# Preparing the experts' weights inside the attention steps of a two-layer transformer kernel on one core

## The chip, the core and the metric

One core of a Trainium2 chip runs the whole program in one launch. The metric is device time in microseconds (us). TensorE is written PE (its weight loads PEld), VectorE DVE, ScalarE ACT, GpSimd POOL; SyncE (SP) issues most DMAs.

## The reference

Input x is 4 x 1024 x 256 (4096 tokens). Each of two layers does a modulated layer norm, attention with 16 heads of 16, a gated residual, a second modulated norm, eight experts of which each token takes two, and a gated residual.

```
h = layernorm(x) * (1 + ca) + sa
x = x + ga * attention(h)        # layer 0: window of 64, q and k rms-normed; layer 1: causal, rope
h = layernorm(x) * (1 + cb) + sb
x = x + gb * experts(h)
# layer 0, for each expert i (H = 1024), tokens with i in their top 2:
W1 = w1_v[i] / max(|row|, 1e-12) * w1_g[i] ;  W2 likewise
out += silu(xm @ W1.T + b1[i]) @ W2.T + b2[i]
# layer 1 (H = 512): gelu(z @ W1 + b1) @ W2 + b2, weighted by the top-2 probabilities
```

The weights are multiplied in two f16 parts: `hi = f16(w)` and `lo = f16(w - hi)`. Layer 0's row norms are not put into the weights but into scales `s1` (on the hidden units) and `s2` (on the outputs).

## The kernel before

`build` runs, for each layer, `project` (norm, q, k, v to DRAM), `attend`, `out_project` and `moe`. Each stage is one block: its engines' programs start together and the next block begins when all have ended. Inside a block each engine follows its own written order and waits on semaphores.

`attend` does 16 steps (4 batches x 4 groups of heads). A list `plan`, made from the sizes, fixes the order inside a step: score matmuls ("st"), maxima of the next step's scores ("max"), the transposes "nmT" (the maxima) and "oT" (the output), and the products with V ("pv"). PE writes "max", "nmT" and "oT" into a ring of two PSUM slots, `pmx`, that DVE empties (`dve_max` L832, `dve_nm`, `dve_norm`); PE may fill a slot only when DVE has read what was in it two entries before. ACT takes the exponentials (L880). SP issues, per step, 13 loads of Q, K and V (L687, L689), after the last "pv" of the step before, and then three small DMAs (L695) that carry the maxima of the next step; that step's scores wait for these. POOL does nothing in the steps.

`moe` runs `moe_input` (norm, router logits, the input z to DRAM in two f16 parts, L1419; ACT writes the first part at L1459 into two buffers, each free again when its store has landed), `moe_route` (who goes where, in chunks of a one-hot product), `moe_weights`, `moe_tiles` (39 tiles of 256 rows) and `moe_combine`.

`moe_weights` is a stage of its own. SP loads an expert's W1 and W2 in f32, ACT copies them to f16 (`hi`) and, in layer 0, squares them (L1238, L1243); PE sums the squares over partitions with a matrix of ones (L1269, L1277); DVE forms `lo` (L1292, L1294) and the scales. Everything stays in `self.w1`, `self.w2`, `self.s1`, `self.s2` in SBUF. Then `moe_tiles` gathers its first rows (L1797), transposes them (L1827), and DVE's copy of them (L1920) lets the first product (L1841) begin.

## Time and profile before

| | |
|---|---|
| three runs | 2458.42, 2462.68, 2467.8 us; median 2462.68 |
| the profiled execution | 2462.16 us, span 2460.3 us |
| busy over the span | PE 74%, DVE 64%, ACT 46%, POOL 25% |
| granted TensorE clock, mean | 0.845 of full speed |

The span is the time from the first to the last instruction of that one execution. The busy shares are means over stages that are bound by different things, so they don't say what a change in one stage is worth; the timeline of that stage does.

### The profile page before, as it was taken

To read this page: it belongs to the slowest core of one execution; us is meant where nothing else is said; L and a number is where in the kernel's file an instruction comes from. 1 tells how busy PE (TensorE), PEld (TensorE's weight loads), DVE (VectorE), ACT (ScalarE), POOL (GpSimd) and SP (SyncE) were. 2 spreads that over 40 slices of the span, in tenths; PEclk is the share of its full clock that TensorE was granted. 3 is DMA by queue.
4 is the path that set the end of the run, shared out by engine and by line. 5 is a ranking of instruction groups with operands and counts; after the bars stand their busy time and mean duration, and the time that the engine had idled before them with its cause. 6 is when DMAs were issued, how large, how long until landed. Compare 5 with 4: busy or idle time off the path is not lost. (4 is left out here: it accounts for less than half of the span.)

```text
span 2460.3 us, 53785 instructions
## 1 busy us (share of the span) xinstructions
PE 1823.6 (74%) x17980; PEld 1306.3 (53%) x17981; DVE 1570.8 (64%) x2726; ACT 1123.6 (46%) x2192; POOL 608.6 (25%) x518
## 2 busy tenths in 40 slices
PE   4994989843688999999159689989887142199990
PEld 2773555643577999899135234433335132177770
DVE  3653777577355566566359589989865797355554
ACT  2662555442553434444035267767784441233332
POOL 0442000023003333333326500000000233155654
PEclk8996999955668999999579789999999555599995
DMA  4324332010531111111423421211100111422226
GB/s 138 115 108 137 100 100 78 16 61 29 203 105 61 50 46 49 47 47 43 154 81 147 154 58 46 65 48 46 46 3 16 48 42 38 146 75 80 80 75 219
DMA packets 160130, 196.79 MB, mean 80 GB/s; under 512 B 23188, under 2 KB 122676, under 8 KB 159460
## 3 DMA queue, kind: packets, MB, share of 16 engines
q1 hardware_dynamic: 144792, 153.72, 19.6%
q0 software_dynamic: 14976, 40.91, 5.5%
q8 instruction: 100, 1.64, 0.3%
q14 instruction: 58, 0.48, 0.1%
q10 hardware_dynamic: 204, 0.05, 0.0%
HBM read 125.97 MB, written 67.67 MB: 79 GB/s over the span
## 5 line engine op out<-in xcount | busy, mean ns | idle before, releaser
L832 DVE TENSOR_REDUCE a_mx<-a_pmx 128x4 f32<-128x512 f32 (+1 forms) x448 | 457.6, 1057 | 88.8 <-PE a_pmx L783 65.5
L880 ACT ACTIVATE a_probs<-a_pst 128x512 f32<-128x512 f32 (+2 forms) x832 | 421.9, 562 | 202.1 <-PE a_pst L799 165.4
L1841 PE MATMUL m_ph<-m_xT,m_w 128*128 128x256 f16 x2808 | 323.2, 275 | 20.8 <-DVE m_xT L1920 20.8
L1855 PE MATMUL m_py<-m_w,m_hh 128*128 x2808 | 319.3, 273 | 0.2 <-issue 0.2
L1841 PEld LDWEIGHTS m_ph<-m_xT,m_w 128*128 x2808 | 273.1, 99 | 63.7 <-issue 30.5
L1855 PEld LDWEIGHTS m_py<-m_w,m_hh 128*128 128x128 f16 x2808 | 268.3, 98 | 35.3 <-issue 2.4
L812 PE MATMUL a_pacc<-a_probs,a_V 128*32 128x256 f32 (+4 forms) x3456 | 247.2, 368 | 0.7 <-ACT a_probs L880 0.3
L1803 POOL DMA_INDIRECT m_y_d<-m_y,m_give x156 | 154.3, 989 | 345.4 <-DVE m_y L1916 329.7
L1926 DVE CAST m_hh<-m_hf 128x512 f16<-128x512 f32 x234 | 101.9, 436 | 210.0 <-ACT m_hf L1891 108.9
L1889 ACT ACTIVATE m_hf<-m_ph,m_b,m_s 128x256 f32<-128x256 f32 x312 | 157.2, 561 | 126.6 <-PE m_ph L1841 117.2
L1797 POOL DMA_INDIRECT m_xr<-z_d,m_take x156 | 152.1, 975 | 224.2 <-issue 221.9
L771 PE MATMUL a_pmx<-a_Ks,a_Qs 48*128 48x192 f16 (+4 forms) x1280 | 167.2, 309 | 52.0 <-DMA a_V<-v_d 36.3
L1380 POOL MEMSET m_eps<- 128x1 f32 x2 | 0.2, 103 | 792.4 <-POOLq L1057 792.4
L793 PE MATMUL a_pst<-a_Qs,a_Ks 51*128 51x192 f16 (+4 forms) x1280 | 157.8, 301 | 32.2 <-ACT a_probs L880 13.7
L1928 DVE TENSOR_TENSOR m_hh<-m_hf,m_hh 128x512 f16<-128x512 f32 x234 | 162.1, 693 | 8.0
L793 PEld LDWEIGHTS a_pst<-a_Qs,a_Ks 51*128 51x128 f16 x1280 | 44.2, 94 | 181.7 <-ACT a_probs L880 139.0
L555 PE MATMUL p_pqk<-p_hT,p_w 128*128 128x512 f32 x256 | 125.9, 615 | 0.0
L812 PEld LDWEIGHTS a_pacc<-a_probs,a_V 128*32 128x32 f32 x3456 | 71.0, 109 | 69.3 <-issue 33.8
L1827 PE MATMUL m_pt<-ident_h,m_xr 128*128 128x128 f16 x624 | 49.3, 224 | 75.3 <-DMA m_xr<-z_d,m_take 75.3
L1891 ACT ACTIVATE m_hf<-m_ph,m_b 128x256 f32<-128x256 f32 x156 | 63.4, 473 | 90.2 <-PE m_ph L1841 88.9
L524 PE MATMUL p_ptr<-ident,p_xn 128*128 128x128 f32 x128 | 27.5, 299 | 97.1 <-DVE p_xn L448 97.1
L771 PEld LDWEIGHTS a_pmx<-a_Ks,a_Qs 48*128 48x128 f16 x1280 | 52.7, 96 | 84.9 <-issue 45.5
(227 smaller groups left out, 3097.4 us busy)
## 6 DMA issues: line engine op xcount, KB each, us to landing
v_d<-p_vt SPq DMA_DIRECT2D x16, 1024.0 KB, 4.6
parts_d<-p_part SPq DMA_DIRECT2D x64, 256.0 KB, 2.6
a_V<-v_d SPq DMA_DIRECT2D x32, 512.0 KB, 3.9
m_got<-m_y_d SPq DMA_DIRECT2D x32, 512.0 KB, 5.8
a_Qs<-parts_d SPq DMA_DIRECT2D x192, 64.0 KB, 2.2
a_Ks<-parts_d SPq DMA_DIRECT2D x192, 64.0 KB, 2.2
z_d<-m_zh SPq DMA_DIRECT2D x16, 512.0 KB, 2.9
m_st<-L_w1T SPq DMA_DIRECT2D x8, 1024.0 KB, 4.8
```

What stands on the lines that cost most here:

```text
L555: mm = nc.tensor.matmul(pqk[:, q % 2, :], w[:, c, ch * P:(ch + 1) * P], hT[:, half, c, :], start=(c == 0), stop=(c == DC - 1))
L771: mm = nc.tensor.matmul(pmx[:, slot, r, n * cols:(n + 1) * cols], Qs[par][ROW2 * r:ROW2 * r + KROWS, p, i * P:(i + 1) * P], Ks[par][ROW2 * ...
L793: mm = nc.tensor.matmul(pst[:, bank(hg, 2 * n + r), off:off + q1 - q0], Ks[par][ROW2 * r:ROW2 * r + KAUG, p, j * P:(j + 1) * P], Qs[par][R ...
L812: mm = nc.tensor.matmul(pacc[32 * h:32 * h + 32, q0 - c * HALF:q1 - c * HALF], V4[par][:, j, h, :], src, start=(v, k) == half_start[c], st ...
L832: nc.vector.tensor_reduce(mx[:, part, :, ps[0]:ps[0] + len(ps), i], src, AX.X, ALU.max).then_inc(m_done, 1)
L880: nc.scalar.activation(probs[:, (hg * NV + g) % NGB, 2 * a + u % 2, 0:w], pst[:, bank(hg, u), 0:w], ACT.Exp, scale=HD ** -0.5).then_inc(ex ...
L1797: pool.indirect_dma_start(xr[:, j % 2, a, :], None, self.z_d[layer][:, :], bass.IndirectOffsetOnAxis(ap=self.take[:, 2 * j + a:2 * j + a + ...
L1803: pool.indirect_dma_start(self.y_d[:, :], bass.IndirectOffsetOnAxis(ap=self.give[:, 2 * j + a:2 * j + a + 1], axis=0), y[:, j % 2, a, :], ...
L1841: mm = nc.tensor.matmul(ph[:, (G * par + g) % 4, q * ROWS:(q + 1) * ROWS], self.w1[:, bass.ds(e, 1), c, wp, m * P:(m + 1) * P].rearrange(" ...
L1855: mm = nc.tensor.matmul(py[:, a, 0:D], hh[:, par, m, hp, a * P:(a + 1) * P], self.w2[:, bass.ds(e, 1), m, wp, :].rearrange("p a n -> p (a ...
L1889: nc.scalar.activation(hf[:, g % 2, q, :], ph[:, (G * par + g) % 4, q * ROWS:(q + 1) * ROWS], func, bias=col(self.b1), scale=col(self.s1)) ...
L1928: nc.vector.tensor_tensor(lo, hf[:, g % 2, :, :], hi, ALU.subtract).then_inc(lo_done, 1)
```

## The change

`moe_weights` is gone. The preparation is spread over the 16 steps of each layer's attention, one of an expert's two matrices per step (even steps W1, odd steps W2): SP loads it in f32 (`load_w`) into `wst`, POOL casts it to `hi`, and `lo` is formed by POOL in layer 1 and by DVE in layer 0, in two halves at items ("lo", 0) and ("lo", 1) of the plan. Both parts are stored to a new DRAM tensor `w_d` (`store_w`). In layer 0, ACT squares the matrix in four pieces after exponentials 3, 5, 7 and 9 of the step, POOL adds the pieces up (one addition of 1024 elements for W1; 1024, 512 and 256 for W2), PE sums over partitions in a new ring item ("sum") of the next step (8 products for W1, one for W2), and DVE copies the sums to `s1` or `s2`.

`moe_input` loads the prepared parts, 16 DMAs, ahead of its own stores of z; `x_d` is stored there too. `moe_route` works in 8 chunks with two buffers each, instead of 4 chunks with one each, to make room. `moe_tiles` turns the sums into scales at its start (root, maximum, reciprocal, product). The weights are 16.8 MB in layer 0 and 8.4 MB in layer 1.

```diff
@@ attend: the plan and the new helpers
+            sum_at = (3, 0) if layer == 0 else None
...
+                if (g, a) == sum_at:
+                    plan.append(("sum",))
+                if layer == 0 and g in (4, 6):
+                    plan.append(("lo", g // 2 - 2))
...
+            def pe_sum(pe, slot, s, hg):
+                par = hg % 2
+                pe.wait_ge(w_acc, s + 1)
+                if par == 0:
+                    for m in range(self.NH):
+                        mm = nc.tensor.matmul(pmx[:, slot, 0, m:m + 1], wsq[:, par, m * P:(m + 1) * P], w_ones[:, 0:1], ...)
+                else:
+                    mm = nc.tensor.matmul(pmx[:, slot, 0, 0:D], w_ones[:, :], wsq[:, par, 0:D], start=True, stop=True)
+                mm.then_inc(w_sum, 1)
...
+            def dve_lo(dve, hg, s, i):
...
+                dve.wait_ge(w_hi, s + 1)
+                nc.vector.tensor_tensor(lo, src, hi, ALU.subtract).then_inc(w_lo, 1)
@@ attend: ACT, in act_step after the exponential u
+                    if layer == 0 and u in (3, 5, 7, 9):
...
+                        nc.scalar.activation(wsq[:, hg % 2, piece], wst[:, hg % 2, piece], ACT.Square).then_inc(w_sq, 1)
@@ attend: POOL, one step
+                        pool.wait_ge(w_in[par], 32 * b + 16 * (hg // 2) + 16)
...
+                        nc.gpsimd.tensor_copy(hi, src).then_inc(w_hi, 1)
+                        pool.wait_ge(w_hi, s + 1)
+                        if layer == 1:
+                            nc.gpsimd.tensor_tensor(lo, src, hi, ALU.subtract).then_inc(w_lo, 1)
+                        if layer == 0:
+                            pool.wait_ge(w_sq, 4 * s + 4)
...
+                                nc.gpsimd.tensor_tensor(wsq[:, par, 0:n], wsq[:, par, 0:n], wsq[:, par, n:2 * n], ALU.add)...
@@ attend: SP, one step (store_w waits for w_lo of the step before)
                     def step(b, hg, last):
                         s = SETS * b + hg
+                        if used(s):
+                            store_w(*((b, hg - 1) if hg else (b - 1, SETS - 1)))
+                        if not last or hg < SETS - 1:
+                            if layer == 0 and used(s):
+                                sp.wait_ge(w_sq, 4 * s)
+                            load_w(*((b, hg + 1) if hg < SETS - 1 else (b + 1, 0)))
                         if not last or hg == 0:
                             if used(s):
                                 sp.wait_ge(pv_done, NX * s)
...
+                    store_w(B - 1, SETS - 1)
+                    for par in range(2):
+                        sp.wait_ge(w_out[par], 16 * STEPS // 2)
@@ moe
-                self.moe_weights(layer)
@@ moe_input: SP, ahead of run(sp, slot)
+                    for e in range(EXPERTS):
+                        for w, dst in enumerate((self.w1, self.w2)):
+                            sp.dma_start(dst[:, e, :, :, :]..., self.w_d[layer][e, w, :, :]).then_inc(self.w_in, 16)
+                    if not twice:
+                        sp.dma_start(self.x_d..., self.x[:, 0:EXPERTS, :]).then_inc(x_out, 16)
@@ moe_route
-            N2, CH = 2 * TILES, 4
+            N2, CH = 2 * TILES, 8
@@ moe_tiles: DVE, ahead of turned(0, 0); before it ACT takes the roots of s1 and s2
+                        for i, (sc, g) in enumerate(((self.s1, g1), (self.s2, b2))):
+                            dve.wait_ge(root, i + 1)
+                            nc.vector.tensor_scalar(sc[:, :, :], sc[:, :, :], 1e-12, None, ALU.max)...
+                            nc.vector.reciprocal(sc[:, :, :], sc[:, :, :])...
+                            nc.vector.tensor_tensor(sc[:, :, :], sc[:, :, :], g[:, :, :], ALU.mult).then_inc(scaled, 1)
```

On DVE, in the second attention step of layer 0 (`a_mx<-a_pmx` is a maximum, `a_nmp` the transposed maxima, `attn` the output), the order before:

```order
L850 TENSOR_TENSOR a_nmp<-a_nmr,a_nmp 32x128
L832 TENSOR_REDUCE a_mx<-a_pmx 128x4 x2
L858 RECIPROCAL a_rden<-a_pmx 128x16
L861 TENSOR_TENSOR attn<-a_pmx,a_rden 128x4x64
L832 TENSOR_REDUCE a_mx<-a_pmx 128x4 x4
```

and now:

```order
L900 TENSOR_TENSOR a_nmp<-a_nmr,a_nmp 32x128
L882 TENSOR_REDUCE a_mx<-a_pmx 128x4
L876 TENSOR_TENSOR a_wpt<-a_wst,a_wpt 128x4x256
L882 TENSOR_REDUCE a_mx<-a_pmx 128x4
L908 RECIPROCAL a_rden<-a_pmx 128x16
L911 TENSOR_TENSOR attn<-a_pmx,a_rden 128x4x64
L882 TENSOR_REDUCE a_mx<-a_pmx 128x4
L876 TENSOR_TENSOR a_wpt<-a_wst,a_wpt 128x4x256
L882 TENSOR_REDUCE a_mx<-a_pmx 128x4 x3
```

The two halves of `lo` (L876) stand between maxima that read different PSUM slots.

On SP, at the start of layer 0's `moe_input`, before:

```order
L1408 DMA m_gg<-L_ffn_gate_g 128x8
L1410 DMA m_rows<-mod_d 128x1024 x2
L1419 DMA z_d<-m_zh 128x4x512 x3
```

and now:

```order
L1372 DMA m_gg<-L_ffn_gate_g 128x8
L1374 DMA m_rows<-mod_d 128x1024 x2
L1389 DMA m_w<-w_d 128x4096 x16
L1391 DMA x_d<-x_res 128x8x256
L1383 DMA z_d<-m_zh 128x4x512 x3
```

Seventeen transfers of 1 MB each stand ahead of the stores of z in the same queue.

On DVE, the first instructions of layer 0's `moe_tiles` (`s` is s1, then s2; `m_xT` the first tiles' rows) are now these, where before the copies of `m_xT` came first:

```order
L1928 TENSOR_SCALAR s<-s 128x64
L1930 RECIPROCAL s<-s 128x64
L1932 TENSOR_TENSOR s<-s,m_g 128x64
L1928 TENSOR_SCALAR s<-s 128x2048
L1930 RECIPROCAL s<-s 128x2048
L1932 TENSOR_TENSOR s<-s,x_res 128x2048
L1914 COPY m_xT<-m_pt 128x1024 x2
```

Six instructions, three of them over 2048 elements, moved ahead of the copies.

## Rows read from the trace of the kernel before

**Rows 1.** Windows: busy us (instructions) of PE, PEld, DVE, ACT, POOL; PEclk, DMA share, GB/s.

```profile
205.00:450.00 245.00, 195.61 (x3792) 125.17 (x3792) 154.29 (x272) 122.22 (x289) 4.40 (x3) 0.90 0.34 92
300.00:352.00 52.00, 45.12 (x881) 29.12 (x881) 35.14 (x61) 27.77 (x67) 0.00 (x0) 0.93 0.36 99
496.00:575.00 79.00, 42.58 (x196) 39.21 (x196) 55.48 (x122) 38.22 (x83) 20.48 (x13) 0.51 0.20 70
617.00:740.00 123.00, 91.76 (x384) 80.05 (x384) 57.68 (x45) 64.24 (x57) 0.20 (x1) 0.65 0.45 154
```

**Rows 2.** Timeline, ends of layer 0's weights stage: start, us, engine, line, op.

```profile
616.56 0.38 SPq L1210 DMA_DIRECT2D x_d<-x_res  x1
...
738.70 0.55 DVE L1313 RECIPROCAL m_s<-m_s 128x64 f32<-128x64 f32 x1
...
739.77 0.35 SPq L1791 DMA_DIRECT2D x_res<-L_ffn_b  x1
...
749.77 12.68 PE L1841 MATMUL m_ph<-m_xT,m_w 128*128 128x256 f16 x96
```

**Rows 3.** Timeline, ends of layer 1's weights stage.

```profile
2085.28 0.38 SPq L1204 DMA_DIRECT2D m_st<-L_ffn_W  x1
...
2136.56 0.35 SPq L1791 DMA_DIRECT2D m_b<-L_ffn_b  x1
```

**Rows 4.** Timeline of SP in a steady attention step of layer 0.

```profile
305.80 2.76 SPq L687 DMA_DIRECT2D a_Qs<-parts_d  x6
...
313.40 1.66 SPq L695 DMA_DIRECT2D a_Qs<-a_nmp  x3
318.48 2.75 SPq L687 DMA_DIRECT2D a_Qs<-parts_d  x6
```

**Rows 5.** Tile m_sq, the squares of the weights: ns min/median/max.

```profile
L1269 PE MATMUL m_pss<-m_ones,m_sq x256: 250/352/367, 627.3 to 728.0; 128*128 128x1 f32 x128
...
L1277 PE MATMUL m_pbc<-m_sq,m_ones x128: 379/634/774, 634.1 to 734.1; 128*128 128x256 f32 x128
L1238 ACT ACTIVATE m_sq<-m_st x16: 1039/1047/1057, 626.1 to 722.0; 128x1024 f32<-128x1024 f32 x16
```

**Rows 6.** Groups by line and shape: busy us, mean ns, idle before.

```profile
L1997 POOL TENSOR_TENSOR m_got<-m_got 128x1024 f32<-128x1024 f32 x8 | 20.1, 2515 | 39.9 <-DMA m_got<-m_y_d 39.9
...
L1294 DVE TENSOR_TENSOR m_w<-m_st,m_w 128x2048 f32 x8 | 18.3, 2292 | 25.5 <-ACT m_w L1244 25.5
...
L1299 DVE RECIPROCAL m_rt<-m_rt 128x256 f32<-128x256 f32 x8 | 14.0, 1753 | 0.3
...
L1294 DVE TENSOR_TENSOR m_w<-m_st,m_w 128x1024 f32 x8 | 9.8, 1225 | 26.5 <-ACT m_w L1244 26.4
...
L1297 DVE TENSOR_SCALAR m_rt<-m_rt 128x256 f32<-128x256 f32 x8 | 2.3, 294 | 9.7 <-ACT m_rt L1250 9.7
```

**Rows 7.** Timeline of the experts' input stage, layer 0.

```profile
498.30 0.91 SPq L1410 DMA_DIRECT2D m_rows<-mod_d  x2
...
514.99 2.12 POOL L1398 TENSOR_TENSOR m_zh<-m_zs,m_zh 128x1024 f16<-128x1024 f32 x1 [17.68 <-ACT m_zh L1459]
...
515.16 3.04 DVE L1541 TENSOR_TENSOR m_zs<-m_zs,m_rows 128x1024 f32<-128x1024 f32 x1
...
517.14 49.18 SPq L1419 DMA_DIRECT2D z_d<-m_zh  x8
...
528.13 1.04 ACT L1459 ACTIVATE m_zh<-m_zs 128x1024 f16<-128x1024 f32 x1
```

**Rows 8.** DMA issues: KB each, median us from issue to landing.

```profile
m_s<-L_ffn_w_g SPq DMA_DIRECT2D x1, 1024.0 KB, 12.1
x_res<-L_ffn_b SPq DMA_DIRECT2D x1, 1024.0 KB, 4.5
```

**Rows 9.** Timeline of SP in the experts' input stage, layer 1.

```profile
1909.02 0.69 SPq L1413 DMA_DIRECT2D m_lnr<-L_ffn_ln_b  x1
1943.38 88.89 SPq L1419 DMA_DIRECT2D z_d<-m_zh  x8
```

More of the change, by code:

```diff
@@ L641, in attend @@
             nm_mid = sem("nm_mid")
+            W = 2 * self.H
+            wst = sb("wst", [P, 2, W])
+            wpt = sb("wpt", [P, 2, 2 * W], F16)
+            wsq = sb("wsq", [P, 2, W]) if layer == 0 else None
+            w_ones = sb("w_ones", [P, P]) if layer == 0 else None
+            w_in, w_out = [sem("w_in0"), sem("w_in1")], [sem("w_out0"), sem("w_out1")]
+            w_set, w_hi, w_lo, w_sq, w_ch, w_acc, w_sum, w_kept = (sem(n) for n in ("w_set", "w_hi", "w_lo", "w_sq", "w_ch", "w_acc", "w_sum", "w_kept"))
             maxu = self.max_units(layer)
@@ L726, in attend @@
             assert not rest
-            ring = [n for n, item in enumerate(plan) if item[0] in ("max", "nmT", "oT")]
+            ring = [n for n, item in enumerate(plan) if item[0] in ("max", "nmT", "oT", "sum")]
             CNT = len(ring)
@@ L732, in runs @@
             def runs(item, hg, first, last):
-                if first and hg == 0 and (item == ("oT", 1) or item[0] == "pv" and item[3]):
+                if first and hg == 0 and (item in (("oT", 1), ("sum",)) or item[0] == "pv" and item[3]):
                     return False
@@ L745, in slot_free @@
                     pe.wait_ge(nmT_read, s + 2)
+                elif item[0] == "sum":
+                    pe.wait_ge(w_kept, s)
                 else:
@@ L944, in _ @@
                     pe.wait_ge(ones_in, 16 * 2 * SETS)
+                    if layer == 0:
+                        pe.wait_ge(w_set, 1)
                     def turn(b, first, last):
@@ L950, in turn @@
                             for n, item in enumerate(plan):
-                                if not runs(item, hg, first, last):
+                                if not runs(item, hg, first, last) or item[0] == "lo":
                                     continue
@@ L976, in _ @@
                     pe_oT(pe, 0, STEPS - 1, 1)
+                    if layer == 0:
+                        pe_sum(pe, 1, STEPS - 1, SETS - 1)
                 @block.vector
@@ L989, in turn @@
                             s = SETS * b + hg
-                            for n in ring:
-                                item = plan[n]
+                            for n, item in enumerate(plan):
+                                if item[0] == "lo":
+                                    dve_lo(dve, hg, s, item[1])
+                                if n not in ring:
+                                    continue
                                 if not runs(item, hg, first, last):
@@ L1008, in _ @@
                     dve_norm(dve, 0, STEPS - 1, 1, TPB * (B - 1) + 4, (SETS - 1) * HG * HD)
+                    if layer == 0:
+                        dve_sum(dve, 1, B - 1, SETS - 1)
                 @block.scalar
@@ L1424, in _ @@
                         sp.wait_ge(zh_out[h], 16 * B)
+                    if not twice:
+                        sp.wait_ge(x_out, 16)
                 @block.scalar
@@ L1645, in _ @@
                         act.wait_ge(col_set, c + 1)
-                        nc.scalar.activation(colv[:, span(c), 0, :], colh[:, span(c), :], ACT.Copy, scale=places[:, 0:1]).then_inc(val1, 1)
+                        if c >= 2:
+                            act.wait_ge(inv_ch, c - 1)
+                        nc.scalar.activation(colv[:, c % 2, :, 0, :], colh[:, c % 2, :, :], ACT.Copy, scale=places[:, 0:1]).then_inc(val1, 1)
                 @block.tensor
@@ L1778, in moe_tiles @@
             ys_ready = sem("ys_ready")
+            g1 = sb("g1", [P, EXPERTS, NH]) if layer == 0 else None
+            g_in, root, scale_ch, scaled = (sem(n) for n in ("g_in", "root", "scale_ch", "scaled"))
             pt = self.ps(ctx, T + "pt", [P, 2, 1024], F16)
@@ L1877, in _ @@
                     act.sem_inc(act_done, 8)
+                    if layer == 0:
+                        nc.scalar.activation(self.s1[:, :, :], self.s1[:, :, :], ACT.Sqrt).then_inc(root, 1)
+                        nc.scalar.activation(self.s2[:, :, :], self.s2[:, :, :], ACT.Sqrt).then_inc(root, 1)
+                        act.wait_ge(scaled, 1)
                     def hidden(j, par):
```

261 lines of the change are left out of this document (100 added, 161 removed).

## The prediction

> **What bounds the kernel now.** The busy shares of the page are read first, and set aside: they mix stages. The windows by stage say more. In layer 0's weights stage (617 to 740 us) PE is busy for 92 of 123 us, but at a granted clock of 0.65 and on nothing but the sums of squares; the DMA share is 0.45 [rows 1]. No tile's product can begin in it. Its bounds are read from the timeline: SP's first issue at 616.56, the next stage's first issue at 739.77, so 123.2 us [rows 2]. Layer 1's stage lasts from 2085.28 to 2136.56, 51.3 us [rows 3]. These 174.5 us stand in series with everything and go; the question is what comes back elsewhere.
>
> Layer 0's attention is where the work goes. A step lasts 12.7 us (SP's first load at 305.80 and again at 318.48 [rows 4]). In 52 us of it PE is busy for 45.1 (87%), DVE for 35.1 (68%, 8.6 us a step), ACT for 27.8 (53%), POOL for nothing [rows 1]. PE has the least room, and it already shares two PSUM slots with DVE. Layer 1's steps only get work on POOL.
>
> **The change part by part.** All times are against the profiled execution, 2462.16 us with a span of 2460.3; the median of the three runs, 2462.68, is the same for this purpose.
>
> *Attention, layer 0, per step.* PE's sums: for W1 eight products with one column, for W2 one of 256 columns. The least durations of their kinds, 250 and 379 ns, are those at the higher clock [rows 5], which this stage has (0.93 [rows 1]). Eight of the first are at most 2.0 us; they overlap, so I take 1.6, and 0.5 us for the second with its weight load, a mean of 1.05, all of it on PE's path.
>
> DVE's halves: two subtractions of 1024 elements at 1.22 us [rows 6]. DVE has 4.1 us idle a step, but not where these stand. The first delays one maximum by 1.2 us and PE's maximum two ring entries later; PE is occupied with the transposes for about half of that, so I charge 0.6. ACT's last square (half of 1.05 us for 1024 elements [rows 5]) delays the same transposes by 0.5 and is in that 0.6. The second half meets POOL's additions, which can start only when the fourth square is done. What then happens is in the input stage: POOL's subtraction ran from 514.99 to 517.11, DVE's product of two SBUF tensors began at 515.16 and took 3.04 us instead of 1.2; it ended 1.1 us after POOL did [rows 7]. So the half waits for the rest of an addition of 2.5 us [rows 6], between 0 and 2.5; I take the middle, 1.2 us, and with the half itself, less the slack of the ring, 1.1 us on PE's next maximum. The Trainium skill ("SBUF — State Buffer", "SBUF: two separate sides") says that DVE with two SBUF inputs and POOL exclude each other for a whole instruction. By that rule the price is the remainder, as above; by a sharing of bandwidth, at the row's ratio of 2.5, it would be 1.8 us each time and the stage 10 us longer.
>
> Sum: 1.05 + 0.6 + 1.1 = 2.75 us a step, 44 us for 16. The stage's end waits for the last half's store, 1 MB behind DVE's last work, 4.5 us [rows 8] less the last products: 2 us. Together 46. Bounds: from below 17 us (only PE's sums are felt; less is excluded, since PE is at 87% and has more to do), from above 8 us a step (1.05, two halves of 1.22 and each a whole addition of 2.5 waited for), 128 us.
>
> What SP gets beside this is two issues a step of 0.4 us and 2.1 MB in its queue. Its chain is nearly closed already: loads from 305.80, the maxima's DMAs from 313.40 to 315.06, and in the 3.4 us until the next step's loads those DMAs land and the scores and products that wait for them run [rows 4]. The store waits for the second half, so it comes at the step's end, where SP waits for the last products anyway. I cost it at nothing as long as the step grows by 2.7 us; it is a rival below.
>
> *Attention, layer 1.* POOL casts and subtracts 1024 elements in a step; DVE's maxima read PSUM, and no row shows such an operation slowed by POOL. 0 us, up to 0.5 a step (8) for the extra issues.
>
> *Input stage, layer 0.* Sixteen loads of 1.05 MB and x_d, 17.8 MB, are issued behind the rows of 498.30, in about 8 us. Before, the first store of z was issued at 517.14, and ACT's third first-part ran at 528.13 [rows 7]; it has to wait for that store's landing, since there are two buffers. In the present trace a transfer of 1 MB issued behind three others landed after 12.1 us instead of 4.5 [rows 8]: one queue is worked off in order. The rate: the weights stage moved 154 GB/s at a share of 0.45 [rows 1], so about 340 GB/s when full. 17.8 MB then take 52 us, from 500 to 552, and the store lands at 554. With rows of 8 KB it could be somewhat faster; 400 GB/s would give 547. I take 551, 23 us behind 528, less 1 us caught up: 22. Bounds: 0 (the store passes the loads) and 30. The Trainium skill ("SBUF — State Buffer", "A bandwidth-pool intuition that's wrong (but worth ruling out)") gives about 358 GB/s for HBM; by that the loads would take 50 us and this term would be 22 to 24, an estimate that this trace neither shows nor excludes.
>
> *Input stage, layer 1.* 8.4 MB from 1909.7 take 25 us, to 1937; the first store of z was issued at 1943.38 [rows 9]. Hidden: 0 us. If that cover were gone (a rate below 250 GB/s), it would cost the difference.
>
> *Routing.* Eight chunks of half the size instead of four: the same elements, eight more instructions on each engine, a shorter tail. 0 us, -2 to +3 in each layer.
>
> *Tiles, layer 0.* The first product began 10.0 us after the stage's first issue (749.77 - 739.77 [rows 2]). Now DVE first waits for 1 MB of w2_g, issued second, landing 4.5 us later [rows 8]: 5.3 us. The scale s1 takes a reciprocal of 0.55 us [rows 2] and two small operations, 1.0. For s2, 2048 elements, the operations were seen on 256: the maximum 0.29 us, the reciprocal 1.75 [rows 6], so at most 2.4 and 14.0; the product as the subtraction over 2048, 2.29 [rows 6]. That is 18.7; with the fixed part of each counted once about 17.5. First product at 5.3 + 1.0 + 17.5 + 0.7 = 24.5 us: 14.5 later than before, at most 16. Layer 1 has no such chain. b2 now comes after the scales and lands 5 us later, under the first tile's 12.7 us of products [rows 2].
>
> The sum: 2462.2 - 174.5 + 46 + 22 + 14.5 = **2370 us**.
>
> **The rivals.** *A: the halves are absorbed.* DVE's 4.1 us of idle time take both halves and only PE's sums count: 17 + 2 us. For it: DVE waits for PE, not the other way round, in most of its gaps, and every delay of PE lets DVE catch up. Against: the idle time lies at the transposes, the halves elsewhere. 2370 - 27 = 2343.
>
> *B: the stores of z don't wait.* If what SP issued later can pass the loads, the input stage costs nothing: 2348. Against it is the landing after 12.1 us.
>
> *C: SP's queue sets the step.* The store waits for a delayed second half; store and load add 0.9 us ahead of the 13 loads, and the maxima's DMAs land behind 2.1 MB more, 6.2 us at 340 GB/s, two thirds of it not under SP's issues: 4.1. The step becomes 12.7 + 5.0: +80, not +44, and the time 2406. For it: SP's issues and the landing after them fill the step already. Against: 9.3 us of issues are room for most of the 6.2.
>
> *D: slower than before.* One chain: second half, store, load, the 13 loads, the maxima's DMAs, the scores, with nothing overlapped. Then the 6.2 us of transfers come in full on top of 12.7, and each half waits for a whole addition (5.0), 11.2 us a step, 179 for 16: 2370 - 44 + 179 = 2505. It decides from 8.5 us a step on, since 174.5 - 22 - 14.5 - 2 = 136 us are left for 16 steps. Against: as for C, and an addition is met at its start in half of the cases at most.
>
> *E: the change doesn't do what it says*, that is, the weights aren't there when the tiles begin. The loads end some 60 us before that. Nothing speaks for it.
>
> **How the numbers follow.** The forecast 0.50; A 0.23; B 0.08; C 0.14; D 0.03; E and what I don't see 0.02. A with B gives 2321, so low is 2336, which leaves out about one in ten; C sets the upper end, 2410. The forecast's own range is 2355 to 2388. About 0.5% (12 us) is what a measurement of this kernel tells from no change. All cases but D and part of the last are far beyond it: faster 0.95, within 0.5% 0.02, slower 0.03.
>
> **What would show it.** The two weights stages are gone and nothing of their length stands between routing and tiles. Layer 0's steps last 15 to 15.5 us; L876 has two kinds of durations, 1.2 us at its first place and up to 3.7 at its second. PE's idle time before the maxima's products names DVE. ACT's third first-part of z stands some 22 us later in its stage than 528.13 did, in layer 0 alone. The copies of m_xT in layer 0's tiles begin 24 us after the stage, behind a reciprocal of about 13 us. I am wrong if the step stays under 14 us (A) or passes 17 with SP late (C), if the input stage is as long as before (B), or if layer 1's steps grew.

## The result, and the profile after

The changed kernel takes 2379.04 us (median of 4 runs, 2373.74 to 2381.89) against 2463.01 us of the kernel before on the same chip: ratio 0.9656, 95% interval 0.9631 to 0.9682, so 84 us less. 2370 us were forecast, 92 us less. The profiled execution took 2377.91 us with a span of 2375.9.

Where it went, stage by stage, from SP's first issue in one stage to its first issue in the next (us; "weights" has no stage after the change):

| stage | before | after | difference | forecast |
|---|---|---|---|---|
| attention, layer 0 | 244.9 | 306.3 | +61.3 | +46 |
| experts' input, layer 0 | 73.4 | 93.7 | +20.3 | +22 |
| routing, layer 0 | 46.9 | 46.7 | -0.2 | 0 |
| weights, layer 0 | 123.2 | - | -123.2 | -123.2 |
| tiles, layer 0 | 445.7 | 459.0 | +13.3 | +14.5 |
| attention, layer 1 | 469.7 | 467.4 | -2.3 | 0 |
| input and routing, layer 1 | 179.6 | 178.6 | -0.9 | 0 |
| weights, layer 1 | 51.3 | - | -51.3 | -51.3 |
| tiles, layer 1 | 270.0 | 268.4 | -1.6 | 0 |

All terms but one came out within 3 us. Layer 0's attention grew by 15 us more than forecast; the small terms together came out 8 us lower, so that the whole is 8 to 9 us off. The windows of the kernel after (busy us and instructions of PE, PEld, DVE, ACT, POOL; PEclk, DMA share, GB/s) answer to [rows 1]:

```profile
205.00:511.00 306.00, 239.62 (x3936) 155.12 (x3936) 204.97 (x320) 155.58 (x353) 95.52 (x52) 0.83 0.63 183
300.00:352.00 52.00, 44.41 (x775) 28.42 (x767) 40.70 (x62) 30.57 (x72) 19.52 (x11) 0.90 0.72 200
557.00:651.00 94.00, 42.65 (x196) 39.22 (x196) 51.78 (x116) 38.36 (x83) 19.39 (x10) 0.51 0.63 247
```

Against the kernel before the granted clock of the attention stage is what stands out: 0.83 where it was 0.90, and in the same 52 us 0.90 where it was 0.93. DMA's share doubled, and DVE is at 67% in the whole stage. The groups of the added instructions in this stage (busy us, mean ns, idle before):

```profile
L876 DVE TENSOR_TENSOR a_wpt<-a_wst,a_wpt 128x1024 f16<-128x1024 f32 x32 | 53.0, 1657 | 0.0
...
L939 ACT ACTIVATE a_wsq<-a_wst 128x512 f32<-128x512 f32 x64 | 40.8, 638 | 0.4 <-DMA a_wst<-L_w1T 0.4
L977 POOL TENSOR_TENSOR a_wsq<-a_wsq 128x1024 f32<-128x1024 f32 x16 | 37.7, 2355 | 172.9 <-ACT a_wsq L939 172.9
...
L855 PE MATMUL a_pmx<-a_w_ones,a_wsq 128*128 128x1 f32 x128 | 15.6, 252 | 0.0
...
L857 PE MATMUL a_pmx<-a_wsq,a_w_ones 128*128 128x256 f32 x16 | 6.4, 487 | 0.0
```

L855 has 128 entries for 8 sums: sixteen matmuls each, not eight, as every f32 product is issued twice. The timeline around one of them (start, us, engine, line, op; in brackets the idle time ahead and what ended it):

```profile
291.51 1.95 PE L855 MATMUL a_pmx<-a_w_ones,a_wsq 128*128 128x1 f32 x16
...
293.50 0.17 DVE L867 COPY s<-a_pmx 128x8 f32<-128x8 f32 x1 [1.81 <-PE a_pmx L855]
...
293.90 0.27 PE L847 MATMUL a_pmx<-ident,a_nm 128*32 128x128 f32 x1 [0.44 <-DVE a_nm L891]
```

The sum takes 1.95 us of PE, and DVE is idle for 1.81 us until it ends. PE alone, 20 to 35 us later:

```profile
312.54 0.66 PE L842 MATMUL a_pmx<-ident,a_oT 128*128 128x128 f32 x4 [0.88 <-ACT a_oT L919]
...
318.35 0.34 PE L794 MATMUL a_pmx<-a_Ks,a_Qs 48*128 48x192 f16 x4 [1.20 <-DVE a_mx L882]
...
320.00 1.07 PE L842 MATMUL a_pmx<-ident,a_oT 128*128 128x128 f32 x4 [0.35 <-ACT a_oT L919]
...
324.67 1.95 PE L855 MATMUL a_pmx<-a_w_ones,a_wsq 128*128 128x1 f32 x16
327.08 0.40 PE L847 MATMUL a_pmx<-ident,a_nm 128*32 128x128 f32 x1 [0.47 <-DVE a_nm L891]
```

PE's first maximum behind the second half waits 1.20 us for DVE, as forecast. But the four transposes that took 0.66 us at 312.54 take 1.07 at 320.00, and the one that took 0.27 at 293.90 takes 0.40 at 327.08: PE's clock has fallen, and it falls again behind the sum. The halves themselves (tile a_wpt: ns min/median/max) last up to 2.63 us, where 3.7 was the most that I had expected:

```profile
L876 DVE TENSOR_TENSOR a_wpt<-a_wst,a_wpt x32: 1202/1214/2626, 247.2 to 503.8; 128x1024 f16<-128x1024 f32 x32
```

What the second half meets on POOL is not what the forecast had in every step. In a step of W1 it falls into POOL's cast of the next matrix, in a step of W2 into the two short additions:

```profile
250.59 1.89 POOL L965 CAST a_wpt<-a_wst 128x2048 f16<-128x2048 f32 x1
250.93 2.63 DVE L876 TENSOR_TENSOR a_wpt<-a_wst,a_wpt 128x1024 f16<-128x1024 f32 x1
...
265.49 5.37 POOL L977 TENSOR_TENSOR a_wsq<-a_wsq 128x1024 f32<-128x1024 f32 x3 [13.01 <-ACT a_wsq L939]
...
268.14 2.14 DVE L876 TENSOR_TENSOR a_wpt<-a_wst,a_wpt 128x1024 f16<-128x1024 f32 x1
```

The first of these halves ends 1.1 us after the cast. In both kinds of step the large addition had ended before the second half began (the three additions of the second case take 2.4, 1.3 and 1.6 us).

Layer 0's input stage, which answers to [rows 7]. The sixteen loads' issues alone last 21.5 us, the first store of z goes out at 584.25, and ACT's third first-part waits 19.85 us for its landing. It stands 52.3 us into its stage; before it was 31.9 (528.13 - 496.22), so 20.4 later:

```profile
560.51 21.52 SPq L1389 DMA_DIRECT2D m_w<-w_d  x16
...
584.25 19.70 SPq L1383 DMA_DIRECT2D z_d<-m_zh  x2
...
609.96 1.06 ACT L1431 ACTIVATE m_zh<-m_zs 128x1024 f16<-128x1024 f32 x1 [19.85 <-DMA z_d<-m_zh]
```

The start of layer 0's tiles, which answers to [rows 2]:

```profile
698.06 0.33 SPq L1778 DMA_DIRECT2D m_g<-L_g1c  x1
...
702.95 0.20 DVE L1928 TENSOR_SCALAR s<-s 128x64 f32<-128x64 f32 x1 [5.38 <-DMA x_res<-L_ffn_w_g]
...
705.18 12.95 DVE L1930 RECIPROCAL s<-s 128x2048 f32<-128x2048 f32 x1
...
718.16 2.29 DVE L1932 TENSOR_TENSOR s<-s,x_res 128x2048 f32<-128x2048 f32 x1
720.37 1.28 DVE L1914 COPY m_xT<-m_pt 128x1024 f16<-128x1024 f16 x2
...
721.20 13.12 PE L1831 MATMUL m_ph<-m_xT,m_w 128*128 128x256 f16 x96 [13.10 <-DVE m_xT L1914]
```

DVE starts 4.9 us after the stage's first issue, the chain of the scales lasts 17.5 us with its reciprocal of 12.95, and the first product begins at 721.20, 23.1 us into the stage (forecast 24.5), 13.1 later than before. Layer 1's stages answer to [rows 3, 9]: routing follows tiles with nothing between, and the first store of z was not held up.

```profile
2004.36 0.36 SPq L1591 DMA_DIRECT2D m_iota<-c_iota  x1
...
2053.82 0.33 SPq L1781 DMA_DIRECT2D m_b<-L_ffn_b  x1
```

### The profile page after: what moved, and what is told of

The parts are those of the page before. It is cut to its first block and busy times, and to the rows that moved or that the text cites. A ratio compares the mean times of both kernels' runs of the same rounds, so it can differ in the third digit from the quotient of the medians.

```text
span 2375.9 us, 53210 instructions
## 1 busy us (share of the span) xinstructions
PE 1775.8 (75%) x17740; PEld 1255.6 (53%) x17741; DVE 1559.7 (66%) x2735; ACT 1080.4 (45%) x2193; POOL 750.6 (32%) x605
## 5 line engine op out<-in xcount | busy, mean ns | idle before, releaser
L1831 PE MATMUL m_ph<-m_xT,m_w 128*128 128x256 f16 x2808 | 324.0, 275 | 33.4 <-DVE m_xT L1914 33.2
L835 PE MATMUL a_pacc<-a_probs,a_V 128*32 128x256 f32 (+4 forms) x3456 | 254.5, 378 | 0.4
L1884 ACT ACTIVATE m_hf<-m_ph,m_b,s 128x256 f32<-128x256 f32 x312 | 157.0, 560 | 127.2 <-PE m_ph L1831 118.4
L965 POOL CAST a_wpt<-a_wst 128x2048 f16<-128x2048 f32 (+1 forms) x32 | 47.8, 1494 | 390.5 <-DMA a_wst<-L_ffn_W 361.8
L977 POOL TENSOR_TENSOR a_wsq<-a_wsq 128x1024 f32<-128x1024 f32 (+2 forms) x32 | 60.6, 1893 | 174.1 <-ACT a_wsq L939 172.9
L1463 PE MATMUL m_plg<-m_gw,m_zT 128*128 128x8 f32 x256 | 57.6, 345 | 61.0 <-ACT m_zT L1434 60.9
```

What stands on the lines that cost most here:

```text
L835: mm = nc.tensor.matmul(pacc[32 * h:32 * h + 32, q0 - c * HALF:q1 - c * HALF], V4[par][:, j, h, :], src, start=(v, k) == half_start[c], st ...
L1831: mm = nc.tensor.matmul(ph[:, (G * par + g) % 4, q * ROWS:(q + 1) * ROWS], self.w1[:, bass.ds(e, 1), c, wp, m * P:(m + 1) * P].rearrange(" ...
L1884: nc.scalar.activation(hf[:, g % 2, q, :], ph[:, (G * par + g) % 4, q * ROWS:(q + 1) * ROWS], func, bias=col(self.b1), scale=col(self.s1)) ...
```

## The experiments

What had to be explained was the 61.3 us of layer 0's attention. Three attention stages that run the very same code (the kernel after and the kernels e7 and e8 below) last 306.3, 303.3 and 309.7 us, so a difference under some 6 us between two single stages says nothing by itself. The useful number is the length of a step in a stretch with a granted clock of 1.00, taken here from DVE's last operation on the maxima (the third row of tile a_nmp) to the same one a step later; of the 14 such intervals behind the first, one spans the return of PE's loop (17.9 us before the change, 24.5 after) and is left out in both columns.

| kernel | stage, us | steps at clock 1.00, us | of 13 intervals, clock below 1.00 |
|---|---|---|---|
| before | 244.9 | 12.7 to 13.0 | 0 |
| after | 306.3 | 16.5, 15.1 | 11 |
| e1, no sum | 273.0 | 14.6, 14.2 | 1 |
| e2, no halves | 289.5 | 15.1, 14.1 | 8 |
| e3, no sum, squares, additions | 265.5 | 13.2 to 13.5 | 2 |
| e4, almost none | 245.8 | 12.7 to 13.1 | 0 |
| e5, small transfers | 310.6 | none | 13 |
| e6, sum behind the transpose | 303.0 | 15.4, 16.1 | 9 |
| e7 and e8, the same attention as after | 303.3, 309.7 | 16.5 to 16.6, 15.1 | 10, 10 |
| e9, one product | 284.4 | 15.0, 15.1 | 2 |
| e10, sum in f16 | 280.7 | 14.9, 14.7 | 4 |
| e11, together | 284.4 | 15.5, 14.9 | 2 |
| e12, halves on POOL | 277.0 | 14.0, 14.5 | 1 |

Two numbers are the step with W1's sum and the step with W2's; in e6 each of W1's sums lies across the border of two intervals, ten matmuls in one and six in the next. A few intervals at full clock are longer than the table's: up to 15.5 us in e1, 16.2 in e2, 14.4 in e3. In e1's of 15.5 us PE waits 1.85 us for the maxima's small DMAs (a_Qs<-a_nmp), which it never does behind the first interval of the kernel after.

**e1, no sum.**

```
-            sum_at = (3, 0) if layer == 0 else None
+            sum_at = None
-                                act.wait_ge(w_sum, s - 1)
+                                act.wait_ge(w_acc, s - 1)
...
+                        pool.memset(self.s1[:, :, :], 1.0)
+                        pool.memset(self.s2[:, :, :], 1.0)
```

> Layer 0's attention without the sum of the squares: the products of L855 on PE, their copy L867 on DVE and the place of both in the ring of PSUM slots are gone; the scales s1 and s2 are set to 1.0 instead, so layer 0's experts are left unscaled. All else stays, the squares and POOL's additions too. The stage lasts 306.25 us with the whole change. My theory now (the sum stands just ahead of the transpose of the maxima, so that DVE, PE and ACT wait for one another there, about 2.5 to 3 us a step): the stage falls by 38 to 48 us, to 258 to 268. The prediction's own term (1.05 us a step): it falls by 17 us, to 289. Rival 'clock' (the steps with a lower granted clock are what is dear, whoever makes them idle): the steps at the full clock stay at 16.0 less 1.05 us, and the 18.6 us steps stay as frequent. The tiles stage stays 459.

Measured: 2350.03 us (ratio to before 0.9536, 0.9517 to 0.9555); the stage 273.0 us, 33.2 less. That lies between the two theories' numbers. Of the step at full clock W1's sum takes 1.9 us and W2's 0.9, a mean of 1.4; 16 times that is 22 us. I put the other 11 us down to the clock: the windows from 240 to 450 us of the kernel after and of this one have

```profile
240.00:450.00 210.00, 177.76 (x3010) 115.80 (x3006) 155.55 (x242) 117.92 (x270) 69.31 (x37) 0.87 0.72 204
```

```profile
240.00:450.00 210.00, 167.01 (x3258) 106.62 (x3260) 173.90 (x261) 132.54 (x303) 75.81 (x40) 0.96 0.78 225
```

0.87 against 0.96. So the clock rival was wrong in saying that the steps would stay as slow and as frequent without the sum, and the 11 us are in line with its other half, that the clock is a cost of its own.

**e2, no halves**, and **e3, no squares, additions and sum.**

```
# e2
-                if layer == 0 and g in (4, 6):
+                if False:
                     plan.append(("lo", g // 2 - 2))
...
-                        sp.wait_ge(w_lo, (SETS * b + hg + 1) * (1 if layer else 2))
+                        sp.wait_ge(w_lo if layer else w_hi, SETS * b + hg + 1 + (0 if layer else 1))
...
# e3, on top of e1
-                    if layer == 0 and u in (3, 5, 7, 9):
+                    if False:
...
-                        if layer == 0:
+                        if False:
```

> Layer 0's attention without VectorE's two halves (L876): the second part of the weights stays zero, the store waits for POOL's cast instead. The sum, the squares and POOL's additions stay. Leaves out layer 0's second weight parts. The prediction's term is 0.6 + 1.1 us a step and 2 us at the end: the stage falls by 29 us, from 306 to 277. My theory now (the sum is the dear part, the halves mostly lie in DVE's idle time): it falls by 8 to 16 us, to 290 to 298. If the lock with POOL costs what the prediction's upper bound says (7 us a step), it falls by far more.

> As the run without the sum, and also without ACT's squares (L939) and POOL's additions (L977); POOL's cast, DVE's two halves, the loads and the stores stay. Leaves out layer 0's scales. What this run is shorter than the one without the sum is the cost of the squares and of the additions with their effect on DVE's halves. My theory now: 0 to 0.5 us a step, up to 8 us, since L876 never lasted over 2.6 us in the trace. The prediction (part of the 0.6 and most of the 1.1 us): 12 to 20 us less than without the sum.

Measured: e2 2365.03 us (0.9592, 0.9573 to 0.9612), its stage 16.8 us shorter than after, just over my 8 to 16 and well under the prediction's 29, and rival A, which had the halves absorbed, is out; e3 2341.02 us (0.9505, 0.9482 to 0.9528), its stage 7.6 us shorter than e1's, within my 8 and under the prediction's 12 to 20. At full clock: the halves 1.4 and 1.0 us a step while POOL has its additions too (after against e2), 0.5 us when it doesn't (e3 against e4), and squares and additions together 1.05 (e1 against e3). The reason is in the groups from 240 to 450 us. Without the additions (e3) and with them (e1) the halves take

```profile
L876 DVE TENSOR_TENSOR a_wpt<-a_wst,a_wpt 128x1024 f16<-128x1024 f32 x28 | 34.2, 1220 | 0.0
```

```profile
L876 DVE TENSOR_TENSOR a_wpt<-a_wst,a_wpt 128x1024 f16<-128x1024 f32 x27 | 47.8, 1770 | 0.0
...
L979 POOL TENSOR_TENSOR a_wsq<-a_wsq 128x256 f32<-128x256 f32 x6 | 9.5, 1583 | 0.5
```

and without the halves (e2) POOL's short addition, which meets the second half, takes

```profile
L979 POOL TENSOR_TENSOR a_wsq<-a_wsq 128x256 f32<-128x256 f32 x6 | 4.4, 730 | 0.5
```

Each lengthens the other: the mean half from 1220 to 1770 ns, the short addition from 730 to 1583. The cast, which the additions push to where it meets a half, keeps its 1.89 us: it begins first.

**e4, almost none**, and **e5, small transfers.** Both shrink the weights' transfers in layer 0's attention:

```
+                        n = W // c // (1 if layer else 16)
+                        sp.dma_start(wst[:, hg % 2, :]....[:, :, 0:n], src[:, :, 0:n])...
...
+                        n = 2 * W // (1 if layer or isinstance(b, int) and b == 0 and hg < 2 else 16)
+                        sp.dma_start(dst[:, 0:n], wpt[:, hg % 2, 0:n])...
...
```

e4 also has the edits of e2 and e3.

> Layer 0's attention with next to nothing of the preparation: no sum, no halves, no squares, no additions; loads and stores are a sixteenth of their size (the first two stores whole), POOL's cast stays; the input stage loads its sixteen pieces all from the first expert's place. If nothing of what stays costs anything (the cast on POOL, two small issues a step on SP), the stage is as before the change, 245 to 248 us. If the waits that the preparation puts into SP's queue cost by themselves, it is longer by that.

> The whole change, but in layer 0's attention the weights' loads and stores are a sixteenth of their size (the first two stores whole); every computation stays, on data left in the buffers, and the input stage loads its sixteen pieces all from the first expert's place. Leaves out layer 0's true weights. If SP's queue and the transfers set the step (rival C of the prediction), the stage falls from 306 to 290 or less. My theory now: transfers cost next to nothing, 303 to 307.

Measured: e4 2321.85 us (0.9423, 0.9407 to 0.9438), the stage 245.8 us; e5 2376.7 us (0.964, 0.9624 to 0.9657), the stage 310.6, not shorter than the others. The window from 240 to 450 us of e5 has a DMA share of half of that above:

```profile
240.00:450.00 210.00, 178.25 (x2930) 115.82 (x2926) 152.38 (x235) 115.29 (x263) 66.31 (x36) 0.85 0.35 95
```

All of e5's intervals are below full clock, so its steps are compared with steps of about the same clock: 18.1 and 15.9 us there (clock 0.88 and 0.92), 18.2 and 15.7 to 16.0 in the kernel after (0.86 to 0.89 and 0.83 to 0.92). Rival C is out: neither the 2.1 MB a step nor SP's waits cost anything in steps of this length. With e5, e4 says that what the change costs in this stage is in the four kinds of work that e4 takes out.

**e6, the sum behind the transpose.**

```
-                if (g, a) == sum_at:
-                    plan.append(("sum",))
...
                     plan.append(rest.pop(0))
+                    if layer == 0 and plan[-1] == ("nmT",):
+                        plan.append(("sum",))
```

> The whole change, with the sum one place later in the order of PE and DVE: behind the transpose of the maxima instead of ahead of it. The same work. My theory (the sum's products delay that transpose and with it DVE's chain on the maxima; behind it they lie under that chain): the stage falls from 306 by 1 to 2 us a step, to 275 to 290, and the kernel by as much. Rival (what counts is only that PE has 2 us more to do): 306 stays within 3 us.

Measured: 2379.45 us (0.9662, 0.9646 to 0.9679), as after; the stage 303.0 us. The place is not what costs, and my theory on it fell. At full clock the mean of its two kinds of step is 15.8 us as before, and 9 of 13 intervals are below full clock all the same.

**e9, one product**, and **e10, the sum in f16.**

```
# e9
-                    for m in range(self.NH):
+                    for m in range(1):
...
# e10
-            w_ones = sb("w_ones", [P, P]) if layer == 0 else None
+            w_ones = sb("w_ones", [P, P], F16) if layer == 0 else None
+            wsh = sb("wsh", [P, 2, self.H], F16) if layer == 0 else None
...
-    nc.gpsimd.tensor_tensor(wsq[:, par, 0:n], ...)
+    nc.gpsimd.tensor_tensor((wsh if last else wsq)[:, par, 0:n], ...)
```

> The whole change, with only the first of the eight columns of W1's sum formed (L855 two matmuls instead of sixteen, 0.25 us instead of 1.95, every second step); the place in the order, the waits and W2's sum (0.7 us) stay. Leaves out seven eighths of s1, which is 1.0. It tells PE's time apart from the place and its waits. If the place and its waits are the dear part (my theory before these runs), the stage keeps 300 us or more. If PE's own time is it, counted once in every second step, it falls by 8 x 1.7 = 14 us, to 292; if the lower granted clock of these steps comes with those products too, to 280 to 286, with the steps that hold the one product at a clock of 1.00 as in the run without the sum.

> The whole change, with POOL's last addition writing f16 and PE's sums of the squares multiplied in f16 (one pass instead of two); same places and waits. A slightly coarser scale of layer 0's experts. PE's part falls from 1.95 and 0.70 us to about 0.9 and 0.3. If PE's time is what costs, the stage falls by 8 x (1.05 + 0.4) = 12 us at least, to 294; with the clock back at 1.00 to 280 to 288. Rival: place and waits, 300 or more.

Measured: e9 2358.57 us (0.9574, 0.9558 to 0.959), its stage 21.9 us shorter; e10 2357.03 us (0.9567, 0.9551 to 0.9583), its stage 25.5 shorter, both within the 280 to 288 us that the return of the clock was to bring. The place, the copy and every wait are still there in both. In e9 the step with W1's sum falls from 16.5 to 15.0 us, by 1.5 where 1.7 us of matmuls went; that is 12 of the 22 us, and the rest goes with the clock, 0.93 in this window against 0.87:

```profile
240.00:450.00 210.00, 169.61 (x3137) 107.93 (x3139) 168.67 (x258) 126.95 (x291) 73.51 (x39) 0.93 0.78 219
```

So PE's own time is what the sum costs, and most of the fallen clock comes with the one-column f32 products of W1: in the six kernels that have all sixteen (after, e2, e5 to e8) 8 to 13 of 13 intervals are below 1.00, in the seven others with the change, 0 to 4.

**e7, the loads spread**, and **e8, the scales split**, for the terms of 20.3 and 13.3 us.

```
# e7
                             sp.dma_start(self.z_d[layer]..., zh[:, h, :, :, :]...)
+                            if not twice:
+                                fetch(n)
...
-                    for e in range(EXPERTS):
...
+                    if twice:
+                        for e in range(EXPERTS):
+                            fetch(e)
# e8
-                        sp.wait_ge(scaled, 2)
+                        sp.wait_ge(scaled2, EXPERTS)
...
+                        scale(0, self.s1, g1, (slice(None), slice(None), slice(None)))
                     turned(0, 0)
                     turned(1, 1)
-                    tile(0, 0)
+                    tile(0, 0, piece)
```

> The whole change, with layer 0's sixteen loads of prepared weights issued two at a time, one expert behind each store of z, instead of all ahead of them. If the queue is worked off in order and the first store of z waits behind 17.8 MB (the prediction's term of 22 us): the input stage falls from 93.7 to 74 to 77 us and the kernel by 17 to 20 us. Rival (what costs is the traffic itself, wherever it stands): the stage stays over 85 us, or the time comes back in the routing or tiles stage.

> The whole change, with layer 0's scales of the tiles stage computed otherwise: s1 first (it waits for its own small load), then the copies of m_xT and the first tile, and s2 in eight pieces of one expert, one behind each pair of rows of the first two tiles. If the chain of 17.5 us ahead of the copies is what the stage grew by (13.3 us): the stage falls from 459 by 9 to 13 us. Rival (the pieces, 1.75 us each for the reciprocal and 0.6 beside, delay DVE's parts of the first tiles as much as the chain delayed the copies): it falls by 0 to 4 us.

Measured: e7 2368.42 us (0.9616, 0.9599 to 0.9632); its input stage 80.6 us, 13.1 less where I had 17 to 20, and routing 1.9 more. Most of the term is the place in the queue, then, and not the traffic. The stores are on time again (the first 22.0 us into the stage, 20.9 before the change), and the third first-part no longer waits. What is left comes at the end: the last store of z stands behind two loads issued just before it, and the stage ends 9.4 us after it (3.7 before):

```profile
578.50 0.39 SPq L1387 DMA_DIRECT2D z_d<-m_zh  x1
...
623.93 1.28 SPq L1381 DMA_DIRECT2D m_w<-w_d  x2
627.64 0.40 SPq L1387 DMA_DIRECT2D z_d<-m_zh  x1
...
637.07 0.33 SPq L1597 DMA_DIRECT2D m_iota<-c_iota  x1
```

e8 2389.7 us (0.9695, 0.9677 to 0.9712), slower than after; its tiles stage is 467.6 us, 8.6 longer instead of shorter. The first product begins 9.6 us into the stage, so the chain was indeed what had delayed it. But the pieces stand between DVE's parts of the tiles, and ScalarE waits for DVE five times, up to 2.49 us; here in the first tile:

```profile
712.28 13.15 PE L1832 MATMUL m_ph<-m_xT,m_w 128*128 128x256 f16 x96
...
718.95 1.75 DVE L1931 RECIPROCAL s<-s 128x256 f32<-128x256 f32 x1
...
721.08 0.42 DVE L1921 CAST m_hh<-m_hf 128x512 f16<-128x512 f32 x1
...
722.37 1.02 ACT L1885 ACTIVATE m_hf<-m_ph,m_b,s 128x256 f32<-128x256 f32 x2 [2.25 <-DVE m_hh L1923]
```

Both of my numbers for it were too good: the rival had the mechanism, not the size. Eight pieces of 2.45 us put 20 us of DVE's time into two tiles.

**e11, together**, and **e12, the halves on POOL.**

```
# e11: e6 and e10, and
...
-                        nc.scalar.activation(self.s1..., ACT.Sqrt)
+                            nc.scalar.activation(sc[:, :, :], sc[:, :, :], ACT.Ln).then_inc(logs, 1)
+                            nc.scalar.activation(sc[:, :, :], sc[:, :, :], ACT.Exp, scale=-0.5).then_inc(root, 1)
...
+                            if not twice and not (isinstance(n, int) and n == 7):
+                                fetch(n + 1)
# e12, on top of it
-                if layer == 0 and g in (4, 6):
+                if False:
...
-                        if layer == 1:
+                        if True:
                             nc.gpsimd.tensor_tensor(lo, src, hi, ALU.subtract).then_inc(w_lo, 1)
```

> The version that the runs point to: the sums in f16, behind the transpose of the maxima; in layer 0's input stage x_d and the first expert's two loads ahead, then one expert's loads behind each of the first seven stores of z; in the tiles stage 1/sqrt of both scales by ScalarE as exp(-0.5 ln x) instead of square root and VectorE's reciprocal of 12.95 us. Sum of the parts, if each holds: attention 306 to 278 to 282 (-26), input 93.7 to 75 to 78 (-17; the run with the loads behind every store had 80.6 and ended late by its last loads), tiles 459 to 447 to 449 (-11): 2379 - 54 = 2325, range 2315 to 2340. If the gains overlap or come back: over 2345.

> As the last, with layer 0's second weight parts formed by POOL in one subtraction of 2048 elements, between its cast and its additions, instead of by VectorE in two halves. POOL then has 1.9 + 4.3 + 5.4 = 11.6 us of work in a step of 14 to 15. If the halves' price is DVE's time on the path (16.8 us in the run without them), attention falls by 10 to 17 us more and the time is 2310 to 2317. If the price moves (POOL late with the additions, so the sum, the store and the next load late): same or slower than the last, 2325 or more.

Measured: e11 2330.05 us (5 runs; 0.945, 0.9437 to 0.9463), 49 us under the changed kernel. Its tiles stage is 445.3 us (13.7 less), its input stage 80.0 (13.7 less: the seventh pair of loads still goes out 3.7 us ahead of the last store), its attention 284.4 (21.9 less); 2325 was expected, with the tiles at 447 to 449, the input at 75 to 78 and the attention at 278 to 282. The chain of the scales is now

```profile
664.16 2.13 ACT L1879 ACTIVATE s<-s 128x64 f32<-128x64 f32 x2
...
667.60 2.06 ACT L1882 ACTIVATE s<-s 128x64 f32<-128x64 f32 x2
...
669.69 2.29 DVE L1941 TENSOR_TENSOR s<-s,x_res 128x2048 f32<-128x2048 f32 x1 [1.44 <-ACT s L1882]
...
671.90 1.28 DVE L1925 COPY m_xT<-m_pt 128x1024 f16<-128x1024 f16 x2
```

and the copies begin 9.1 us into the stage instead of 22.3. e12 takes 2324.95 us (0.943, 0.9415 to 0.9445): 5 us less, the attention 7.4 us less, where I expected 10 to 17. POOL's subtraction lasts 4.1 us beside DVE's maxima, which read PSUM and kept their length (953 ns before the change, 956 here):

```profile
L883 DVE TENSOR_REDUCE a_mx<-a_pmx 128x4 f32<-128x768 f32 x95 | 90.7, 956 | 37.4 <-PE a_pmx L807 36.2
...
L969 POOL TENSOR_TENSOR a_wpt<-a_wst,a_wpt 128x2048 f16<-128x2048 f32 x14 | 57.1, 4076 | 1.1
```

At full clock the step is 14.0 and 14.5 us against 15.5 and 14.9, a mean of 0.95 less, which is 15 us for 16; of the 8 that are missing 5.6 went in the first interval (25.1 us instead of 22.5) and at the loop's return (23.1 instead of 20.1, clock 0.78 against 0.79). In the first interval DVE's small subtraction that ends the maxima, 0.18 us elsewhere, falls into POOL's subtraction and lasts 3.35 us, and PE's transpose stands 3.15 us for it:

```profile
245.01 4.06 POOL L969 TENSOR_TENSOR a_wpt<-a_wst,a_wpt 128x2048 f16<-128x2048 f32 x1
245.76 3.35 DVE L892 TENSOR_SCALAR a_nm<-a_mx 128x32 f32<-128x32 f32 x1
```

Five more of its sixteen take 0.44 to 0.71 us. At the loop's return PE is idle for 7.16 us (3.10 in e11) in which it waits for nothing that the profile shows; why stays open.

## Why the prediction was right, and where it was not

The mechanisms held in the main, and the time is inside the likeliest case's own range. That it is only 9 us off is in part luck: one term was 15 us short, and all the others together came out 8 us under theirs. The removed stages: 174.5 us, as read. Routing, layer 1 and both of its tiles: within 3 us of nothing. The input stage: the store of z had to wait behind 17.8 MB, as the landing of 12.1 us in [rows 8] had suggested; rival B is out. The rate taken from [rows 1] was 340 GB/s; from 560 to 600 us it was 405, above every rate that I had weighed. The seventeenth transfer landed 26.5 us behind its issue at 582.07, so they were in 48 us after the first was issued and not 52. The store was issued later than I had it, 26.6 us into the stage instead of 20.9, behind the loads' own issues, but landed right behind them all the same. 20.3 for 22. The tiles: 13.3 for 14.5, with the reciprocal at 12.95 us against a bound of 14.0; in e11, with a chain of 9.1 us, the stage lasts 445.3 us and before the change 445.7, so nothing else in it had grown.

The term that failed is "44 us for 16" of layer 0's attention steps, with its 2 us for the end: 61.3 were measured for the 46. Of these 56.4 us are in the 14 intervals behind the first (240.4 us against 184.0), 5.4 behind the last interval, and the first one was 0.4 us shorter. The step of the working behind it: "The least durations of their kinds, 250 and 379 ns, are those at the higher clock, which this stage has". It had that clock before the change and lost it with the change. At the full-clock mean of 15.8 us, with the loop's return 5.2 us longer, as before, the 14 intervals would be 226.4 us. So 14.0 of the 56.4 us go with the fallen clock, by an estimate from step lengths that no run isolates, and I had put down nothing for it. The rest is close: 15.8 - 12.8 = 3.0 us a step for the forecast 2.75. The end is another mechanism than I had: the last store is issued at 505.04 and lands 3.9 us later, and the stage ends at 511.22, behind the last sum and its copy, with the clock at 0.79 over these 24 us, where it was 1.00 over the last 19 of the kernel before.

The parts of that 3.0, from the runs, against the forecast's. PE's sums: 1.4 (1.9 and 0.9) for 1.05. This is the count: I took eight products for W1, and they are sixteen matmuls; [rows 5] show it already: L1269 has 256 entries for 8 experts of two chunks of eight products, which are 128. W2's lasts 0.7 us, not 0.5, and both have a copy on DVE (0.17 and 0.42 us), which I left out. Halves, squares and their lock: 1.6 for 1.7, of which the halves alone 0.5. The lock between POOL and DVE was priced by the right rule, and its size came right by luck. The rule: a second half lasts until what POOL has begun is done and then its own time, 2.63 us behind the cast and 2.14 behind the short addition; a sharing at the ratio of 2.5 would have made whole halves 3.0 us long. The luck: I took the middle of an addition of 2.5 us, and up to the last two matrices no second half meets that addition; what is left of the cast (1.9 us) or of the addition of 1.3 us makes a second half 1.1 us longer in the mean (e1 against e3), where I had 1.2. The Trainium skill ("SBUF — State Buffer", "SBUF: two separate sides") says that DVE with two SBUF inputs and POOL exclude each other for a whole instruction; the trace agrees, with POOL's addition of 0.73 us that takes 1.58 in the mean where a half of 1.2 us meets it.

What would have shown the clock in advance? [rows 1] give 0.93 over four steps and 0.90 over the stage, so the stage was not safe from it: before the change the granted clock fell, behind the first interval, at the loop's return only. A change that puts one-column f32 products into such a stage needs a term for it. No row of the kernel before gives its size; the runs do: in the kernel after, the steps in which it fell last up to 18.2 us for 16.5 and 16.4 for 15.1, 1.7 and 1.3 more, so 24 us over 16 steps if all were such. Single steps lost more in other runs (18.1 us for 14.1 in e2, 20.7 for 16.5 in e8).

Three slips of the working changed nothing in the forecast. The upper bound of a step is 1.05 + 2.44 + 5.0 = 8.5 us and not 8, 136 us and not 128. The weights were in some 90 us before the tiles' stage, not 60 (rival E). And steps of over 17 us were to be the sign of rival C; they came, with SP in time, so that sign could not tell C from a fallen clock.

What stays open: why the clock falls in one step and not in the next of the same content. Windows of 2 us of the kernel after and of e9, whose steps lie at nearly the same times, show it:

```profile
316.00:318.00 2.00, 1.09 (x24) 0.49 (x18) 2.00 (x2) 1.39 (x4) 0.34 (x1) 1.00 0.01 4
...
320.00:322.00 2.00, 2.00 (x18) 1.40 (x22) 0.74 (x4) 1.23 (x3) 0.00 (x0) 0.53 0.95 209
```

```profile
316.00:318.00 2.00, 0.75 (x16) 0.43 (x14) 2.00 (x3) 1.30 (x4) 0.00 (x0) 1.00 0.01 4
...
320.00:322.00 2.00, 2.00 (x45) 1.32 (x46) 1.56 (x4) 1.10 (x3) 0.00 (x0) 1.00 0.90 240
```

PE is idle for a part of 316 to 318 in both, in e9 for longer, and only the kernel after is at half the clock from 320 on. What differs in the work before is W1's sum at 291.51. The count over the kernels ties the loss to W1's sixteen matmuls; e10 keeps the single column and changes form, number and time of them at once, so no run says which of these it is.

## What to carry to other kernels

Take the count of matmuls of an f32 product from the rows, not from the loop in the code, and give PE's granted clock a term of its own wherever a change adds narrow f32 products to a stage that runs at full clock. When a stage that you delete sends its loads ahead of another stage's stores in one queue, spread them behind the stores, and not right ahead of the last one. Where GpSimd and VectorE both work in SBUF, read from the trace what GpSimd runs at the moment of each VectorE operation: here it was another operation than planned, and a short one can be held as well as a long one (e12). A chain moved to a stage's start is worth shortening (e11), but cutting it up and strewing it over the engine that has the next work (e8) can cost more than it did in one piece.

## What the runs showed of the hardware

- Eight f32 products with one column are sixteen matmuls in 1.95 us on PE (0.12 each); in f16 they are eight in 0.35 us (0.04 each), and the stage was 25.5 us shorter.
- DVE's subtraction of two SBUF tensors and POOL's short addition lengthen each other (1220 to 1770 ns and 730 to 1583 ns in the mean), and the one that begins second waits: a half begun inside POOL's cast ended 1.1 us behind it, and a DVE operation of 0.18 us begun inside POOL's subtraction took 3.35, while DVE's maxima from PSUM kept their 0.95 us beside POOL's subtraction of 4.1 us.
- SP's issue of a 1 MB load took 0.4 to 0.5 us in an attention step and 1.35 us in a row of sixteen (21.52 us; the median 0.56, the longest 4.14), with the engines at a DMA share of 1.00 and 405 GB/s. That the transfers hold the issuing queue is the likely reading; no run varies it by itself.
- ScalarE's logarithm and exponential over both scales (64 and 2048 elements) take 2.13 and 2.06 us, with 1.28 us ahead of each for its table; VectorE's reciprocal over the 2048 alone took 12.95 us.
